# Down products of two expert layers, part of them in three rounded passes, in a four-layer transformer block on one Trainium2 core

## The chip, the cores and the metric

The kernel runs on one core of one Trainium2 chip. The time is the device time of one execution in microseconds (us). The core's engines are TensorE (PE in the rows; PEld is its weight load), VectorE (DVE), ScalarE (ACT), GpSimd (POOL) and SyncE (SP, which issues most of the transfers). Each engine runs its own instructions in the order in which they were written; engines wait for each other through semaphores only.

## The reference, cut to what matters

The input x is 4 batches of 512 tokens of 128 features, all in float32. Four layers follow each other, each added to x behind a layer norm:

```python
x = x + L0_xattn(layernorm(x), ctx, ctx)   # 16 heads of 8, 154 context rows
x = x + L0_ffn(layernorm(x))               # 8 experts, hidden width 512, top 2, gelu
x = x + L1_xattn(layernorm(x), ctx)        # self attention, cross attention, feed forward, three norms
x = x + L1_ffn(layernorm(x))               # 32 experts, hidden width 64, top 6, silu(g) * u, one shared expert
```

In the first expert layer every expert is computed for every token: `h = gelu(x W1 + b1)`, `y = h W2`, and the outputs are summed with the routing weights, which are zero for experts that were not chosen. In the second one `o = (silu(x Wg) * (x Wu)) Wd`, also for every expert, weighted in the same way. The products with `W2` and `Wd` are the down products.

## The kernel before, in words

The work of one batch is four stages: A (first attention), B (first expert layer), C (second attention with its feed forward) and D (second expert layer). Batches are interleaved: stage A of all four runs first, then B of one batch beside C of the batch before, then D beside what is left of C and D's own router. All products keep features on partitions and the 512 tokens along the free dimension, so that a 128x512 float32 tile fills one PSUM bank.

The order of each engine's instructions is taken from five tables, `PLAN_SP`, `PLAN_POOL`, `PLAN_ACT`, `PLAN_DVE` and `PLAN_PE` (lines 107 to 331). Each names a part of the work (a generator such as `gelus` or `downs`), a batch, and a start for each of its steps; `merged` (L38) writes the steps down in order of these starts. Nothing at run time looks at the starts: they fix the order within an engine, and the semaphore waits do the rest. A planner outside the kernel made the tables.

**Stage B** has 32 chunks of 128 hidden features (`NC0`), four for each expert. For chunk c, `first` (L1655) multiplies by W1 in three passes of a rounded type, `fp32r`: the weights and the input were each split into a rounded high part and the remainder (`product3`, L1491: high by high, low by high, high by low; lines 1493, 1494, 1495 in the rows). The result is in bank 0 or 1. `gelus` (L901, row L911) on ScalarE writes it into one of four slots of `h32`. `second` (L1673, row L1681) multiplies the slot by a 128x128 block of `w2s` in plain float32, accumulating the four chunks of an expert in bank 2. VectorE multiplies bank 2 by the routing weights `WB`, which a transfer spread over all partitions (`stage_b`, L1245, tile `ty`), and GpSimd adds the result to `acc_o` (L776).

**Stage D** has 17 chunks (`ND`): the shared expert and 16 pairs of experts. `gates` (L1825) makes two three-pass products, gate into bank 0 and up into bank 1. ScalarE takes silu of bank 0 into `s32`, two slots (`stage_d`, L1002). VectorE multiplies it by bank 1 into a slot of `h32` (L1445), and for chunks 1 to 16 multiplies the slot by the combine weights `CB` (L1451). `downs` (L1840, row L1851) multiplies by `dns`, or `shd` for chunk 0, in plain float32, and accumulates all 17 chunks in bank 2. Then comes a copy to SBUF, a transposition, the addition of x and the store.

Banks 0 and 1 are claimed anew for each chunk, so that TensorE's next product into bank 1 waits for L1445 of the chunk before.

**Stage C** and the routers are chains of many small steps. A norm (class `Norm`) is, on VectorE, four statistics (L395), four aggregates (L399), then, behind two GpSimd steps (L424, and the power at L427), four steps of 128x4 (L403, L406, L409, L412) and four 128x128 scalings (L418). All of VectorE's work, that of stage D too, stands in one queue with these.

GpSimd's own work is small before the change: the power steps, the sums of stage B, a bias sum (L786) and the low halves of the second layer's gate and up weights (`split1`, L748).

Of the kernel before, what the change touches and what calls it, by code (L numbers as in the profile page):

```python
# [25 lines left out]
F32 = mybir.dt.float32  # L26
F32R = mybir.dt.float32r
U8 = mybir.dt.uint8
ALU = mybir.AluOpType
# [62 lines left out]
class Signal:  # L92
# [6 lines left out]

    def then(self):  # L100

        return Signal(self.sem, self.per, self.at(NB, 0))
# [5 lines left out]
    "constants": [[6, 1272, 10975]],  # L108
    "load_x": [[0], [1040], [2704], [5590]],
    "load_context": [[1260], [4711], [7811]],  # L110
    "second_weights": [[14389, 14395, 28061, 38108, 39646, 41268]],
    "load_context1": [[14407], [24876], [31482], [35078]],
    "store": [[48439], [50521], [56182], [57613]],
    "spread_first": [[13617, 13859, 14401, 14945, 15567, 16098, 16858, 17511, 18133], [18975, 19217, 19342, 20142,
        21401, 22143, 23263, 23892, 24870], [26203, 26446, 26452, 27125, 28055, 28944, 30116, 30829, 31476], [32967,
        33210, 33216, 33959, 35072, 35774, 37822, 38062, 38535]],
    "spread_second": [[37816, 38084, 38096, 38541, 38553, 40408, 40666, 41025, 41256, 41444, 41808, 42078, 42388,
# [4 lines left out]
}  # L122
PLAN_POOL = {
    "constants": [[0, 15, 32, 60, 289, 340, 368]],
    "norm_a": [[710, 737], [1818, 1845], [3788, 3815], [7460, 7487]],
    "values": [[1946], [5119], [8117], [11089]],
    "key_tails": [[1983, 3916], [4316, 5058], [8157, 8218], [9729, 11027]],
    "norm_b": [[6000, 6027], [13177, 13204], [18984, 19787], [26163, 26191]],
    "stage_b": [[14945, 15567, 16098, 16858, 17511, 18133, 18858, 19342], [21045, 21401, 22143, 23263, 24803, 24939,
# [204 lines left out]
def build_program(nc, a):  # L334
# [5 lines left out]
    def sig(name, per):  # L340
        return Signal(ctx.enter_context(nc.semaphore(name)), per)
# [1599 lines left out]
```

## Time and profile before

| | |
|---|---|
| median of 3 runs | 597.2 us (596.64 to 597.66) |
| the profiled execution | 596.67 us |
| its span, first to last instruction | 594.9 us |
| TensorE busy | 569.7 us (96%) |
| VectorE busy | 401.7 us (68%) |
| ScalarE busy | 322.5 us (54%) |
| GpSimd busy | 105.4 us (18%) |
| transfers | 38.35 MB, 64 GB/s in the mean |

Matmuls are pipelined and their recorded ends are modelled: a row of TensorE starts with the weight load's end and overlaps the next. What a pass costs is read from start to start, or from the chain of waits, which counts each stretch once. A plain float32 product of 128x512 appears as two records, a three-pass product as three. VectorE rows may overlap a little as well.

### The profile page before, as it was taken

The numbers are of one execution on the slowest core, as the hardware profiler recorded it, in microseconds if no ns is written. First come the engines' busy times: TensorE is split into PE (matmuls) and PEld (weight loads), VectorE is DVE, ScalarE is ACT, GpSimd is POOL, SyncE is SP. The second block draws the span as 40 slices with busy tenths as digits, with TensorE's granted clock in tenths as the row PEclk, the third lists the DMA queues.
The fourth block names the chain that finished last, engine by engine and source line by source line (L and its number), as shares of the span: only waits on it lengthen the run. The fifth ranks groups of instructions, "written<-read, shape, count | busy, mean of one in ns | idle before, by whom it ended". The sixth has DMA issues, their size and how long they took to land.

```text
span 594.9 us, 8098 instructions
## 1 busy us (share of the span) xinstructions
PE 569.7 (96%) x2512; PEld 374.7 (63%) x2512; DVE 401.7 (68%) x1265; ACT 322.5 (54%) x566; POOL 105.4 (18%) x120
## 2 busy tenths in 40 slices
PE   4899999999999999999999899999899999999997
PEld 3556666665566667656676466666666676666664
DVE  6888989774132344666637585777889999768564
ACT  1587688766454476644855348745292542342321
POOL 3111110000111311242202432126201110100000
PEclk9999999999999999999999999999899999999999
DMA  4400000300311100101111011061321233341431
GB/s 119 195 15 10 18 10 2 105 39 19 107 36 35 54 20 19 36 28 54 60 31 44 14 42 44 1 199 39 122 75 51 90 119 98 111 138 62 143 120 56
DMA packets 23306, 38.35 MB, mean 64 GB/s; under 512 B 3776, under 2 KB 9536, under 8 KB 22880
## 3 DMA queue, kind: packets, MB, share of 16 engines
q1 hardware_dynamic: 22832, 37.44, 19.9%
q8 instruction: 20, 0.33, 0.2%
q10 hardware_dynamic: 432, 0.40, 0.2%
q14 instruction: 22, 0.18, 0.1%
HBM read 36.45 MB, written 1.38 MB: 64 GB/s over the span
## 4 chain that ended last, share of the span: by engine, by line
PE 80%; DVE 10%; ACT 4%; issue 2%; POOL 2%; DMA 1%; DVEq 0%; POOLq 0%; ACTq 0%
PE ps L1681 16%; PE ps L1493 9%; PE ps L1495 9%; PE ps L1851 9%; PE ps L1494 9%; PE ps L1488 3%; PE ps L1568 3%; PE ps L1588 3%; PE ps L1500 3%; PE ps L1603 2%; PE ps L1600 2%; PE ps L1758 1%; PE ps L1738 1%; DVE NM L1156 1%; PE ps L1530 1%
## 5 line engine op out<-in xcount | busy, mean ns | idle before, releaser
L1493 PE MATMUL ps<-xThi,w1s 128*128 128x512 f32 x256 | 147.5, 576 | 2.9 <-DVE h L1445 2.6
L911 ACT ACTIVATE h<-ps,early 128x512 f32<-128x512 f32 x128 | 86.7, 687 | 88.8 <-PE ps L1495 68.9
L1681 PE MATMUL ps<-h,w2s 128*128 128x512 f32 x256 | 122.5, 594 | 3.3 <-DVE ty L1245 3.2
L1495 PE MATMUL ps<-xTlo,w1s 128*128 128x512 f32 x256 | 101.4, 396 | 0.0
L1494 PE MATMUL ps<-xThi,w1s 128*128 128x512 f32 x256 | 100.9, 394 | 0.0
L1002 ACT ACTIVATE s<-ps 128x512 f32<-128x512 f32 x68 | 40.7, 598 | 95.4 <-PE ps L1495 93.8
L1493 PEld LDWEIGHTS ps<-xThi,w1s 128*128 128x128 f32 x256 | 48.5, 190 | 37.3 <-issue 18.2
L1681 PEld LDWEIGHTS ps<-h,w2s 128*128 128x128 f32 x256 | 46.2, 189 | 35.5 <-issue 23.8
L1494 PEld LDWEIGHTS ps<-xThi,w1s 128*128 128x128 f32 x256 | 48.7, 190 | 28.6 <-issue 24.3
L776 POOL TENSOR_TENSOR acc_o<-acc_o,ty 128x512 f32<-128x512 f32 x32 | 41.9, 1310 | 140.2 <-DVE ty L1245 115.7
L1445 DVE TENSOR_TENSOR h<-s,ps 128x512 f32<-128x512 f32 x68 | 46.5, 684 | 28.2 <-PE ps L1495 21.0
L1851 PE MATMUL ps<-h,w2s 128*128 128x512 f32 x128 | 63.5, 592 | 0.0
L1156 DVE TENSOR_REDUCE NM<-ps 128x2 f32<-128x308 f32 x128 | 56.1, 471 | 10.5 <-PE ps L1568 9.2
L1245 DVE TENSOR_TENSOR ty<-ps,WB 128x512 f32<-128x512 f32 x32 | 22.0, 686 | 53.4 <-PE ps L1681 53.4
L1495 PEld LDWEIGHTS ps<-xTlo,w1s 128*128 128x128 f32 x256 | 48.3, 189 | 11.2
L1451 DVE TENSOR_TENSOR h<-h,CB 128x512 f32<-128x512 f32 x64 | 44.2, 690 | 1.0
L1568 PE MATMUL ps<-KS,QS 128*128 128x320 f32 x128 | 41.8, 375 | 2.2 <-DVE NM L1156 1.4
L864 ACT ACTIVATE h<-ps 128x512 f32<-128x512 f32 x54 | 31.1, 597 | 10.8 <-PE ps L1588 9.7
L1568 PEld LDWEIGHTS ps<-KS,QS 128*128 128x128 f32 x128 | 23.6, 194 | 18.4 <-DVE NM L1156 9.7
L1851 PEld LDWEIGHTS ps<-h,w2s 128*128 128x128 f32 x128 | 23.8, 189 | 11.1 <-issue 5.3
L1588 PE MATMUL ps<-QS,KS 128*128 128x512 f32 x64 | 26.2, 440 | 0.4
L798 ACT ACTIVATE QS<-ps 128x512 fp32r<-128x512 f32 x32 | 18.4, 596 | 11.3 <-PE ps L1500 11.0
(264 smaller groups left out, 889.6 us busy)
## 6 DMA issues: line engine op xcount, KB each, us to landing
CB<-ct_rows SPq DMA_DIRECT2D x128, 128.0 KB, 2.9
WB<-wt_rows SPq DMA_DIRECT2D x32, 256.0 KB, 3.2
w2s<-w_dram SPq DMA_DIRECT2D x2, 2048.0 KB, 8.5
raw<-gu_dram SPq DMA_DIRECT2D x4, 512.0 KB, 3.8
x_in<-x_dram SPq DMA_DIRECT2D x4, 256.0 KB, 2.9
w2s<-dn_dram SPq DMA_DIRECT2D x1, 1024.0 KB, 5.7
out_dram<-ty SPq DMA_DIRECT2D x4, 256.0 KB, 2.9
late<-late_dram SPq DMA_DIRECT2D x1, 608.5 KB, 7.5
```

What stands on the lines that cost most here:

```text
L776: nc.gpsimd.tensor_tensor(acc_o[:], acc_o[:], ty[:, e % 2, :], ALU.add).then_inc(b_acc.sem, 1)
L911: nc.scalar.activation(h32[:, c % HR, :], bank[c % 2], ACT.Gelu, bias=b1T[:, c:c + 1]).then_inc(b_gelu.sem, 1)
L1156: V.tensor_reduce(NM[:, i, h:h + 2], src, AX.X, ALU.max, negate=True).then_inc(a_nm.sem, 1)
L1445: V.tensor_tensor(h, s32[:, (b * ND + n) % 2, :], bank[1], ALU.mult).then_inc(d_t.sem, 1)
L1451: V.tensor_tensor(h, h, CB[:, slot, :], ALU.mult).then_inc(d_h.sem, 1)
L1493: M(dst, w[0], xThi[:, x, :], start=start, stop=False)
L1494: M(dst, w[1], xThi[:, x, :], start=False, stop=False)
L1495: return M(dst, w[0], xTlo[:, x, :], start=False, stop=stop)
L1568: M(bank[u % 2][:, 0:2 * KW], QS[:, g, i * P:(i + 1) * P], KS[:, g, 2 * half:2 * half + 2, :].rearrange("p h k -> p (h k)"), start=True, s ...
L1588: M(bank[k], lhs, QS[:, g, :], start=True, stop=True).then_inc(a_s_ps.sem, 1)
L1681: M(bank[2], w2s[:, c * P:(c + 1) * P], h32[:, c % HR, :], start=(c % 4 == 0), stop=(c % 4 == 3)).then_inc(b_y.sem, 1)
L1851: M(bank[2], w, h32[:, (b * ND + n) % HR, :], start=(n == 0), stop=(n == ND - 1)).then_inc(d_dn.sem, 1)
```

## The change

The down products of chunks 1, 3, 5, ... of stage B and all down products of stage D are made in three passes of rounded parts instead of one plain float32 product. Even chunks of stage B stay as they were.

For that the hidden tile is split each time: ScalarE copies the 128x512 slot of `h32` into a rounded tile (`highs_b`, `highs_d`; two slots each), and GpSimd subtracts it from the slot, in place, into the remainder (`lows_b`, `lows_d`). The down product waits for the remainder instead of for gelu or for the combine weights. The down weights are split once in the same way: for stage B the odd blocks (`split2`, two pieces of 1024 columns), for stage D the shared block and four pieces of 512 columns (`split3`).

No large tile is added for the high halves: `hh0` (stage B) lies in the memory of `s32`, `hh1` (stage D) in that of `WB`, the low parts in that of `h32`, `w2s` and `shd` themselves (`twins`). So the first silu of stage D waits for the last down product of stage B, and the first high half of stage D for the last use of `WB`. The semaphores are those of parts that ended, counted on.

All five plan tables are replaced by new ones, with the new steps in them; they are left out here. In the new order of TensorE in the last batch of stage D, the down product of chunk n-3 stands behind the gate and up products of chunk n; before it was that of chunk n-2.

```diff
+    def twins(name, shape):
...
+        with nc.sbuf_tensor(name, shape, F32) as plain:
+            pass
+        return plain, sb(name + "_r", shape, F32R)
...
-    h32 = sb("h32", [P, 4, S])
+    h32, h32r = twins("h32", [P, 4, S])
...
-    w2s = sb("w2s", [P, NC0 * P])
+    w2s, w2r = twins("w2s", [P, NC0 * P])
...
+    w2h = sb("w2h", [P, NP1 * P], F32R)
...
-    WB = sb("WB", [P, 2, S])
-    s32 = sb("s32", [P, 2, S])
+    WB, hh1 = twins("WB", [P, 2, S])
+    s32, hh0 = twins("s32", [P, 2, S])
...
+        def split2():
+            for k in range(2):
+                yield
+                pool.wait_ge(w2_hi.sem, w2_hi.at(0, k + 1))
...
+        def lows_b(b):
+            for j in range(NC0 // 2):
+                yield
+                pool.wait_ge(b_hi.sem, b_hi.at(b, j + 1))
+                o = (2 * j + 1) % HR
+                nc.gpsimd.tensor_tensor(h32r[:, o, :], h32[:, o, :], hh0[:, j % 2, :].bitcast(F32), ALU.subtract).then_inc(b_lo.sem, 1)
+
+        def lows_d(b):
+            for n in range(ND):
+                yield
+                t = b * ND + n
+                pool.wait_ge(d_hi.sem, d_hi.at(b, n + 1))
+                nc.gpsimd.tensor_tensor(h32r[:, t % HR, :], h32[:, t % HR, :], hh1[:, t % 2, :].bitcast(F32), ALU.subtract).then_inc(d_lo.sem, 1)
...
+        def highs_b(b):
+            for j in range(NC0 // 2):
+                yield
+                act.wait_ge(b_gelu.sem, b_gelu.at(b, 2 * j + 2))
+                if b or j >= 2:
+                    act.wait_ge(b_y.sem, b_y.at(b, 2 * j - 2))
+                copy(hh0[:, j % 2, :], h32[:, (2 * j + 1) % HR, :]).then_inc(b_hi.sem, 1)
+
+        def highs_d(b):
+            for n in range(ND):
+                yield
+                t = b * ND + n
+                if n:
+                    act.wait_ge(d_h.sem, d_h.at(b, n))
+                else:
+                    act.wait_ge(d_t.sem, d_t.at(b, 1))
+                if t >= 2:
+                    act.wait_ge(d_dn.sem, d_dn.at(b, n - 1))
+                else:
+                    act.wait_ge(b_ty.sem, b_ty.at(NB - 1, E0))
+                copy(hh1[:, t % 2, :], h32[:, t % HR, :]).then_inc(d_hi.sem, 1)
...
+                else:
+                    act.wait_ge(b_y.sem, b_y.at(NB, 0))
                 nc.scalar.activation(s32[:, (b * ND + n) % 2, :], bank[0], ACT.Silu).then_inc(d_silu.sem, 1)
...
+        def down3(dst, w, x, start, stop):
+            (whi, wlo), (xhi, xlo) = w, x
+            M(dst, whi, xhi, start=start, stop=False)
+            M(dst, wlo, xhi, start=False, stop=False)
+            return M(dst, whi, xlo, start=False, stop=stop)
...
-                pe.wait_ge(b_gelu.sem, b_gelu.at(b, c + 1))
-                M(bank[2], w2s[:, c * P:(c + 1) * P], h32[:, c % HR, :], start=(c % 4 == 0), stop=(c % 4 == 3)).then_inc(b_y.sem, 1)
+                j, at, ends = c // 2, c % 4 == 0, c % 4 == 3
+                if c % 2:
+                    pe.wait_ge(b_lo.sem, b_lo.at(b, j + 1))
+                    if b == 0 and j % 8 == 0:
+                        pe.wait_ge(w2_lo.sem, w2_lo.at(0, j // 8 + 1))
+                    w = w2h[:, j * P:(j + 1) * P], odd_low[:, j, :]
+                    down3(bank[2], w, (hh0[:, j % 2, :], h32r[:, c % HR, :]), at, ends).then_inc(b_y.sem, 1)
+                else:
+                    pe.wait_ge(b_gelu.sem, b_gelu.at(b, c + 1))
+                    M(bank[2], w2s[:, c * P:(c + 1) * P], h32[:, c % HR, :], start=at, stop=ends).then_inc(b_y.sem, 1)
...
-                w = shd[:] if n == 0 else dns[:, (n - 1) * P:n * P]
-                M(bank[2], w, h32[:, (b * ND + n) % HR, :], start=(n == 0), stop=(n == ND - 1)).then_inc(d_dn.sem, 1)
+                if b == 0 and (n == 0 or n % 4 == 1):
+                    pe.wait_ge(dn_lo.sem, dn_lo.at(0, 1 + (n + 3) // 4))
+                pe.wait_ge(d_lo.sem, d_lo.at(b, n + 1))
+                c, t = slice((n - 1) * P, n * P), b * ND + n
+                w = (w2h[:, c], dn_low[:, c]) if n else (shh[:], sh_low[:])
+                down3(bank[2], w, (hh1[:, t % 2, :], h32r[:, t % HR, :]), n == 0, n == ND - 1).then_inc(d_dn.sem, 1)
```

## Rows read from the trace of the kernel before

**Rows 1.** Busy time of each engine, share of the span, instructions.

```profile
PE 569.7 (96%) x2512; PEld 374.7 (63%) x2512; DVE 401.7 (68%) x1265; ACT 322.5 (54%) x566; POOL 105.4 (18%) x120
```

**Rows 2.** The chain of waits, 560 to 595 us: start, length, what.

```profile
561.28 0.23 PE ps L1493
561.51 0.23 PE ps L1494
561.75 0.23 PE ps L1495
...
564.91 0.86 PE ps L1851 x2
...
567.15 0.86 PE ps L1851 x2
...
587.38 2.70 PE ps L1851 x6
590.10 0.61 ACT acc_o L798
```

**Rows 3.** Busy time by stretch, all engines: length, then busy and instructions of each.

```profile
135.00:197.00 62.00, 61.46 (x228) 36.87 (x229) 15.58 (x56) 33.17 (x51) 10.52 (x10) 1.00 0.16 49
197.00:266.00 69.00, 67.95 (x285) 44.27 (x284) 36.54 (x121) 41.89 (x73) 17.51 (x17) 1.00 0.10 32
...
461.00:508.00 47.00, 46.54 (x202) 32.64 (x201) 43.94 (x135) 19.84 (x36) 5.44 (x7) 1.00 0.32 97
508.00:550.00 42.00, 42.00 (x162) 28.35 (x161) 31.13 (x87) 14.57 (x23) 1.61 (x2) 1.00 0.35 110
```

**Rows 4.** Groups by line and shape, whole span: busy, mean ns, idle before.

```profile
L798 ACT ACTIVATE QS<-ps 128x512 fp32r<-128x512 f32 x32 | 18.4, 596 | 11.3 <-PE ps L1500 11.0
...
L1451 DVE TENSOR_TENSOR h<-h,CB 128x512 f32<-128x512 f32 x64 | 44.2, 690 | 1.0
```

**Rows 5.** GpSimd's groups by shape, 197 to 461 us.

```profile
L776 POOL TENSOR_TENSOR acc_o<-acc_o,ty 128x512 f32<-128x512 f32 x25 | 32.9, 1317 | 92.8 <-DVE ty L1245 68.3 <-ACT acc_o L798 24.4
...
L748 POOL TENSOR_TENSOR w1s<-raw,w1s 128x1024 fp32r<-128x1024 f32 x4 | 9.9, 2487 | 25.0 <-ACT w1s L798 25.0
...
L786 POOL TENSOR_TENSOR norm2b<-norm,late_rows 128x512 f32<-128x512 f32 x3 | 3.8, 1276 | 5.9 <-DVE norm L1255 5.9
```

**Rows 6.** Timeline, all engines, 417 to 422 us.

```profile
417.43 2.38 POOL L748 TENSOR_TENSOR w1s<-raw,w1s 128x1024 fp32r<-128x1024 f32 x1
417.49 2.34 DVE L403 TENSOR_TENSOR ln_c_t<-ln_c_y 128x4 f32<-128x4 f32 x1 [0.18 <-POOL ln_c_y L427]
...
419.87 0.16 DVE L406 TENSOR_TENSOR ln_c_t<-ln_c_t,ln_c_ve 128x4 f32<-128x4 f32 x1
...
421.35 0.79 PE L1493 MATMUL ps<-xThi,w1s 128*128 128x512 f32 x1 [1.68 <-DVE h L1445]
```

**Rows 7.** The chain of waits, 412 to 426 us.

```profile
422.14 0.43 PE ps L1494
422.57 0.43 PE ps L1495
```

**Rows 8.** Timelines of VectorE, then of GpSimd, from 218.5, 266, 444 and 482.5 us.

```profile
218.74 2.06 DVE L418 TENSOR_SCALAR xn<-X,ln_b_mv,ln_b_t 128x128 f32<-128x128 f32 x4
...
445.41 1.89 DVE L1388 TENSOR_TENSOR sfc<-sc,late_rows 128x128 f32<-128x128 f32 x1
...
482.96 0.69 DVE L1445 TENSOR_TENSOR h<-s,ps 128x512 f32<-128x512 f32 x1
483.87 0.95 DVE L1451 TENSOR_TENSOR h<-h,CB 128x512 f32<-128x512 f32 x1
...
482.98 1.29 POOL L786 TENSOR_TENSOR norm2b<-norm,late_rows 128x512 f32<-128x512 f32 x1 [6.39 <-DVE norm L1255]
...
266.52 1.65 POOL L776 TENSOR_TENSOR acc_o<-acc_o,ty 128x512 f32<-128x512 f32 x1 [4.04 <-DVE ty L1245]
```

**Rows 9.** Who TensorE waited for, 197 to 461 us: total, times, longest.

```profile
PE ps L1681 <- DVE ty L1245: 3.2, 2, 2.1
PE ps L1493 <- DVE h L1445: 2.6, 2, 1.7
PE ps L1777 <- DVE PN L1317: 0.4, 1, 0.4
```

More of the change, by code:

```diff
@@ L107 @@
 PLAN_SP = {
[L108 to L116, printed above, removed]
@@ L258 @@
+    "halves_d": [[35274, 37351], [42230, 43094], [45447, 48114], [50279, 50379]],
+    "router": [[35761, 35793, 35825, 35867, 36042, 36240, 36272, 36323, 36391, 36494, 36526, 36558, 36805, 36825],
[3 rows of a table added]
+    "stage_d": [[39385, 39551, 39673, 39738, 39917, 39980, 40052, 40301, 40423, 40489, 40560, 40696, 41114, 41179,
[8 rows of a table added]
 }
 PLAN_PE = {
-    "context_keys": [[720], [1948], [5240], [8257]],
-    "context_values": [[1150], [4648], [7748], [10485]],
-    "inputs": [[1040, 1237], [2576, 3058], [5600, 6147], [8706, 9088]],
@@ L316 @@
[L316 to L317 removed]
[8 rows of a table removed]
[L326 removed]
[4 rows of a table removed]
+    "context_keys": [[720], [1825], [5405], [8261]],
+    "context_values": [[1150], [4626], [7736], [10507]],
+    "inputs": [[1040, 1239], [2644, 3072], [5234, 6123], [8387, 9133]],
@@ new lines @@
+    "output": [[5329, 5530], [8456, 8656], [11246, 11515], [14086, 14280]],
+    "prepare_b": [[11367, 12094, 13507], [14828, 16240, 19114], [21734, 23034, 24559], [28414, 28779, 30083]],
+    "first": [[13367, 13856, 14131, 14208, 14533, 14602, 14757, 14996, 15065, 15223, 15515, 15584, 15810, 15879, 16103,
[8 rows of a table added]
+    "weights": [[13997], [20919], [26816], [32818]],
+    "second": [[14375, 14464, 14671, 14928, 15137, 15292, 15360, 15446, 15656, 15742, 15948, 16034, 16401, 16487,
[8 rows of a table added]
+    "stage_c": [[14884, 17507, 19217, 20062, 20246, 21479], [26332, 26700, 26905, 26991], [33220, 33296, 33458, 34502]
+        , [39175, 40326, 40521, 41811]],
@@ L434, in build_program @@
     w1s = sb("w1s", [P, 2, NC0 * P], F32R)
-    w2s = sb("w2s", [P, NC0 * P])
+    w2s, w2r = twins("w2s", [P, NC0 * P])
     w1raw = w2s
-    gus, dns = w1s, w2s[:, 0:NP1 * P]
+    w2h = sb("w2h", [P, NP1 * P], F32R)
+    odd, odd_low = (w.rearrange("p (c two k) -> p c two k", two=2, k=P)[:, :, 1, :] for w in (w2s[:], w2r[:]))
+    gus, dns, dn_low = w1s, w2s[:, 0:NP1 * P], w2r[:, 0:NP1 * P]
     shs = sb("shs", [P, 2, 2 * P], F32R)
-    shd = sb("shd", [P, P])
+    shd, sh_low = twins("shd", [P, P])
+    shh = sb("shh", [P, P], F32R)
     lg = sb("lg", [P, NT, E0])
@@ L911, in gelus, with split2, split3 @@
                 nc.scalar.activation(h32[:, c % HR, :], bank[c % 2], ACT.Gelu, bias=b1T[:, c:c + 1]).then_inc(b_gelu.sem, 1)
+        def split2():
+            for k in range(2):
+                yield
+                act.wait_ge(down0_loaded.sem, 16)
+                c = slice(1024 * k, 1024 * k + 1024)
+                copy(w2h[:, c].rearrange("p (c k) -> p c k", k=P), odd[:, 8 * k:8 * k + 8, :]).then_inc(w2_hi.sem, 1)
+        def split3():
+            for k in range(NDN):
+                yield
+                w, hi, _, chunks = down1_piece(k)
+                act.wait_ge(down1_loaded.sem, 32)
+                if chunks:
+                    act.wait_ge(b_y.sem, b_y.at(NB - 1, chunks))
+                copy(hi, w).then_inc(dn_hi.sem, 1)
+        def highs_b(b):
+            for j in range(NC0 // 2):
+                yield
+                act.wait_ge(b_gelu.sem, b_gelu.at(b, 2 * j + 2))
[4 more added lines that the diff above has]
+            for n in range(ND):
+                yield
+                t = b * ND + n
[8 more added lines that the diff above has]
+                copy(hh1[:, t % 2, :], h32[:, t % HR, :]).then_inc(d_hi.sem, 1)
         def stage_c(b):
```

258 lines of the change are left out of this document (139 added, 119 removed), and 196 rows, old and new, of tables (PLAN_ACT, PLAN_DVE, PLAN_PE, PLAN_POOL).

## The prediction

> **What bounds the kernel now.** I read the busy times first: TensorE stands at 96%, the next engine at 68% [rows 1]. That share is of modelled, overlapping records, so I went to the chain of waits for the true pace. In its last 35 us nearly everything is TensorE: a plain float32 down product takes 0.86 us, each of the three rounded passes 0.23 us, so three passes 0.69 us, and two down products that follow each other (564.91 and 567.15) are 2.24 us apart, which is 0.86 + 2 x 0.69 with nothing left over [rows 2]. TensorE alone bounds the last stage. By stretches the other engines have room in places: VectorE is busy for 15.6 of 62 us in the first stage B, for 36.5 of 69 in the next with stage C beside it, for 43.9 of 47 in the second stage D with the end of C and a router beside it, and for 31.1 of 42 in the third [rows 3]. Last I looked at what TensorE waits for from 197 to 461 us: VectorE, in few but long waits [rows 9]. Two of the longest lead to one cause, and it decides this prediction.
>
> **That cause.** At 417.43 GpSimd begins a subtraction of 2.38 us that reads SBUF. VectorE's next step, a product of 128x4 elements in SBUF, begins at 417.49 and lasts 2.34 us; the one behind it, of the same size, takes 0.16 us. VectorE's queue is held, stage D's product L1445 stands in it, bank 1 stays taken, and TensorE is idle for 1.68 us [rows 6]. Its passes then take 0.43 instead of 0.23 us until 424 us [rows 7]: the granted clock fell from the level of 2.4 GHz to that of 1.2 GHz behind the idle time, which costs another 6 x 0.2 + 0.2 = 1.4 us. So one GpSimd instruction cost the end some 3 us. It isn't alone: a scaling group of four lasts 2.06 us where four undisturbed ones last 1.1, a 128x128 sum 1.89 us [rows 8]. Going through VectorE's instructions from 197 to 461 us I find 18 (these two groups hold the first and nearly the last, 218.74 to 445.41) that are longer than others of their line and shape, together by 17.0 us, each beside one of 32 GpSimd instructions that read large tiles: 25 sums, four subtractions of 1024 columns, three bias sums [rows 5]. That is 0.53 us of VectorE for each such GpSimd instruction. The Trainium skill has this as a rule (SBUF — State Buffer, Who interferes with whom): a VectorE instruction with two SBUF inputs and a GpSimd instruction that reads SBUF want the same port pair, and the later one blocks until the other is done. The trace agrees, with 2.34 against 0.16 us. By the same rule an instruction that has one input in PSUM is spared, and the trace agrees there too: L1445 took its usual 0.69 us beside GpSimd's bias sum, while L1451 behind it, both inputs in SBUF, took 0.95 [rows 8]. Without the rule's spared instructions the sum below would be worse.
>
> **The change, part by part.** The sum is made against the profiled execution (596.67 us, span 594.9); the median is 0.5 us above it, so differences are added to 597.2.
>
> TensorE: 64 down products in stage B (16 odd chunks, 4 batches) and 68 in stage D (17, 4 batches) go from 0.86 to 3 x 0.23 us. 132 x 0.165 = 21.8 us less.
>
> ScalarE: 132 copies into a rounded tile at 0.60 us [rows 4], 79 us, and some 6 us for the weights. From 322.5 it comes to about 408 of 600 us [rows 1]; beside B and C it has 41.9 of 69 us, with 16 copies 51.5 [rows 3]. It is covered in the steady part: nothing. If it weren't, a late gelu or silu would cost up to 0.6 us each time.
>
> GpSimd: 132 subtractions of 128x512. The nearest row is the bias sum and the sums at 1.28 to 1.32 us [rows 5]. So 170 us, and the weights' seven, of which two of 1024 columns at 2.4 us, about 10. From 105 to 285 us: it has the time, its port is the question.
>
> The way from the hidden tile to its down product grows by a copy and a subtraction, 0.60 + 1.28 and two waits of 0.05 to 0.1, some 2.0 us. In the steady part of stage D the new order puts the down product three chunks behind, and one chunk is 3 x 0.69 = 2.07 us of TensorE, so this is hidden. It shows at the end: now TensorE makes its last three down products back to back from 587.38 [rows 2]; then the last waits for copy and subtraction. 2.0 less 0.17: +1.9 us. At the start of stage B the first odd chunk is late by as much, with other work in front: between 0 and 2, I take 1. Stage D can't have its first silu until stage B's last down product is done, since both use one memory; stage C's products are there to fill: between 0 and 2, I take 1. The splitting of the weights lies before both and off TensorE: 0. Without the port this gives -21.8 + 1.9 + 1 + 1 = -17.9 us.
>
> The port: stage B of the first batch (VectorE a quarter busy) and stage D of the last (no C beside it) I count as nothing. In the latter a chunk asks the port for L1451, 0.69, and a subtraction, 1.28: 1.97 of 2.07 us, and rows overlap a little at their ends, so it fits. This leaves 48 subtractions of stage B, 51 of stage D and five of the weights, 104, in stretches where VectorE has chains of steps. At 0.53 us each they hold VectorE for 55 us more. What of this reaches the end? Before, 17.0 us of holding went with 7.0 us of TensorE's waits between 197 and 461 us (the three largest rows are 6.2 of them [rows 9]) and the 1.4 us of slow clock: a share of 0.5. So 55 x 0.5 = +27.5 us. Bounds: if only waits as long as the two longest count (3.8 us of 17, a share of 0.22), +12; if VectorE has no room left, as in the second stage D where it already has 43.9 of 47 us, the share goes towards 0.8, +44. I take 0.5, which is measured on the kernel that is nearest, and since slack that absorbs one hold is used up by the next I see no reason to go lower. The other direction, GpSimd held by VectorE, is 0.33 us (1.65 in [rows 8] against 1.32 in the mean [rows 5]), a sixth of a chunk; I take it as covered by the distance of three chunks.
>
> Sum: -17.9 + 27.5 = +9.6, so 606.8 us.
>
> **The rivals.** *Cover holds (faster).* The holds fall into VectorE's idle time, the orders are new and might put the steps of C away from the subtractions. For it: 18 holds led to only four or five visible waits. Against: semaphores, not the order, decide when a subtraction meets a step, and a norm's power step stands on GpSimd itself, so that a subtraction queued right behind it starts exactly when VectorE's next step does, as at 417.43. With a share of 0.1 the price is 5.5: 597.2 - 17.9 + 5.5 = 584.8 us. It decides the sign from a share of 17.9 / 55 = 0.33 downwards.
>
> *VectorE becomes the bound beside C and the routers (slower still).* In the second stage D VectorE would have 43.9 us of work and 17 holds in 43 us of TensorE's. If in the first two stages D each of 34 subtractions holds it for 0.8 us and all of it counts, +27, with the other 70 as above, 70 x 0.53 x 0.5 = +18.5: 597.2 - 17.9 + 45.7 = 625 us. For it: 43.94 of 47 [rows 3]. Against: a part of these holds hits queues with nothing urgent.
>
> *The late halves decide.* Each odd down product waits for its subtraction by 0.3 us because GpSimd's queue also holds sums and power steps of 1.3 and 1.0 us in front of it, and TensorE finds nothing behind it in its own queue: 99 x 0.3 = 30 us on top of -17.9, without port holds: 609 us. Near my number with another cause; the waits view tells them apart.
>
> **How the numbers follow.** My forecast has a chance of 0.57 (its own range 600 to 618), late halves 0.07, VectorE as the bound 0.12, cover holds 0.19, and 0.05 that price and saving cancel. What a measurement can tell from no change is 0.2%, 1.2 us. Faster 0.19, same 0.05, slower 0.76. The range goes from 588 (a share of 0.16) to 625 (the second rival) and leaves out most of "cover holds" and the far end of the second.
>
> **What would show it.** Right: in the last stage D down products are 2.07 to 2.1 us apart; GpSimd is near 285 us; VectorE's small steps (L403, L406, L409, L1388) have means several times 0.16 us, L1451 in stages D with C beside it is over 0.8 us in the mean, and VectorE's busy time rises by some 50 us over 401.7 though no work is added to it; TensorE's waits name VectorE's L1445 and L1245, and the clock falls in more places than one. Wrong: small steps keep their lengths; or they grow and TensorE's waits stay near 7 us from 200 to 460, then the cover holds and the kernel is faster; or three passes of the mixed operands take more than 0.69 us, which no row of before shows for a moving tile written by GpSimd.

## The result and the profile after

The changed kernel takes 636.69 us in the median of four runs (636.22 to 637.21), the kernel before 596.93 in four runs beside it: a ratio of 1.0664, with a 95% interval of 1.0646 to 1.0682, or 39.7 us more. The forecast was 606.8, its range 588 to 625: the sign was right, the size was not, and the time lies outside the range.

First the page of the changed kernel, busy times and granted clock. They answer to [rows 1].

```profile
PE 565.9 (89%) x2644; PEld 399.1 (63%) x2644; DVE 470.9 (74%) x1265; ACT 398.9 (63%) x703; POOL 289.4 (46%) x259
...
PEclk9899999999999999999999999988999989899999
```

TensorE has 3.8 us less to do and falls from 96% to 89% of the span. The 3.8 is not the price of the passes: records at half the clock are longer, and there are more of them now. VectorE has 69 us more, with as many instructions (1265) as before: nobody gave it work. The groups show where it went (line, engine, operation, tile, count; busy, mean ns; idle before).

```profile
L830 POOL TENSOR_TENSOR h_r<-h,WB_r 128x512 fp32r<-128x512 f32 x68 | 93.0, 1377 | 76.5 <-ACT WB_r L880 76.2
L823 POOL TENSOR_TENSOR h_r<-h,s_r 128x512 fp32r<-128x512 f32 x64 | 82.3, 1288 | 104.1 <-ACT s_r L880 104.0
...
L1574 DVE TENSOR_TENSOR h<-h,CB 128x512 f32<-128x512 f32 x64 | 59.2, 925 | 1.2
...
L1568 DVE TENSOR_TENSOR h<-s,ps 128x512 f32<-128x512 f32 x68 | 46.3, 680 | 12.0 <-PE ps L1618 9.5
...
L438 DVE TENSOR_TENSOR ln_n_t<-ln_n_y 128x4 f32<-128x4 f32 x12 | 8.3, 688 | 8.7 <-POOL ln_n_y L462 8.7
...
L453 DVE TENSOR_SCALAR normed<-a,ln_n_mv,ln_n_t 128x128 f32<-128x128 f32 x48 | 24.7, 568 | 0.1
```

L823 and L830 are the new subtractions. L1574 is L1451 of [rows 4]: 690 ns there, 925 here. A product of four columns, L438 (before L403), has a mean of 688 ns; before it had 294, and [rows 6] has an undisturbed step of this size at 0.16 us. L1568 (before L1445), which takes one input from PSUM, keeps its 680 ns.

The stretches come next: length, busy time and count of TensorE, its weight load, VectorE, ScalarE and GpSimd, clock, DMA. They are the four stages B and then the four stages D; [rows 3] has the first two and the sixth and seventh of before.

```profile
140.00:198.00 58.00, 55.84 (x232) 38.13 (x231) 17.48 (x44) 40.88 (x63) 31.52 (x26) 1.00 0.13 42
198.00:266.00 68.00, 63.30 (x292) 44.85 (x292) 42.94 (x110) 47.36 (x87) 33.52 (x30) 1.00 0.13 40
266.00:336.00 70.00, 67.00 (x305) 47.18 (x304) 44.22 (x144) 48.85 (x88) 40.04 (x38) 1.00 0.14 42
336.00:420.00 84.00, 72.22 (x315) 49.69 (x314) 62.14 (x178) 55.23 (x95) 45.40 (x41) 0.96 0.20 66
420.00:489.00 69.00, 55.70 (x258) 41.23 (x257) 64.22 (x158) 41.30 (x76) 40.98 (x33) 0.98 0.15 46
489.00:545.00 56.00, 47.46 (x209) 35.58 (x208) 53.74 (x122) 26.41 (x43) 27.67 (x22) 0.95 0.28 89
545.00:588.00 43.00, 40.61 (x172) 29.56 (x172) 38.77 (x88) 24.48 (x40) 24.22 (x19) 0.99 0.32 99
588.00:635.00 47.00, 40.68 (x173) 30.45 (x171) 31.18 (x38) 22.79 (x38) 26.80 (x20) 0.99 0.32 101
```

The same points of the program in both traces: the first product of each of the four stages B and of the four stages D (taken where its second weight load starts), and the end.

```
          B0     B1     B2     B3     D0     D1     D2     D3     end
before  139.7  197.0  265.6  330.4  405.2  460.8  507.8  549.1  594.9
after   140.5  198.3  266.3  336.3  420.1  488.8  545.2  588.4  635.2
later     0.8    1.3    0.7    5.9   14.9   28.0   37.4   39.3   40.3
```

The first two stages B give back what the holds take. The loss of 36.7 us falls from the third stage B to the end of the second stage D. VectorE is busy there for 44.2 us of 70, then for 62.1 of 84, 64.2 of 69 and 53.7 of 56. The two stages that the forecast counted as free of holds, the first B and the last D, lose 0.5 and 1.0 us, but they aren't free of them: in the last stage D eight of VectorE's 16 combine products (L1574) take 1.1 to 1.7 us instead of 0.69.

What a hold looks like, at its worst (timeline, all engines, 428.5 to 434.5 us):

```profile
428.27 1.28 POOL L857 TENSOR_TENSOR acc_o<-acc_o,ty 128x512 f32<-128x512 f32 x1 [1.13 <-DVE ty L1368]
428.77 3.58 DVE L453 TENSOR_SCALAR normed<-a,ln_n_mv,ln_n_t 128x128 f32<-128x128 f32 x4
429.50 1.29 POOL L816 TENSOR_TENSOR w2s_r<-w2s,w2h 128x512 fp32r<-128x512 f32 x1
430.75 1.26 POOL L830 TENSOR_TENSOR h_r<-h,WB_r 128x512 fp32r<-128x512 f32 x1
...
432.27 0.68 DVE L1568 TENSOR_TENSOR h<-s,ps 128x512 f32<-128x512 f32 x1
433.00 0.72 PE L1616 MATMUL ps<-xThi,w1s 128*128 128x512 f32 x1 [1.99 <-DVE h L1568]
```

Three large reads of GpSimd stand back to back: an old sum, a weights' subtraction, a new one. Four scalings, 1.12 us when nothing disturbs them (at 7.91 us in the trace of before), take 3.58. Stage D's product is behind them in VectorE's queue, and TensorE idles for 1.99 us. Behind this idle the granted clock is 0.5 (the level of 1.2 GHz) for 3.4 us. Apart from the last microseconds of the span that is so six times, at 20.1, 395.6, 412.6, 433.1, 508.2 and 542.3 us; before it was so once, at 421.3 [rows 7]. The stretch at 20.1 us lies ahead of all new work. The others begin near the end of idles of 1.8 to 3.9 us. Not every such idle is followed by one:

```profile
451.02 0.50 PE L1616 MATMUL ps<-xThi,w1s 128*128 128x512 f32 x1 [2.42 <-DVE h L1568]
451.36 0.40 PE L1617 MATMUL ps<-xThi,w1s 128*128 128x512 f32 x1
```

Behind 2.42 us of idle the next pass has its 0.40 us here; in the slow stretch from 433.1 us the same line has 0.63.

Who TensorE waited for over the whole span (total, times, longest):

```profile
PE ps L1616 <- DVE h L1568: 17.7, 18, 2.4
...
PE ps L1818 <- DVE ty L1368: 5.2, 2, 3.9
PE ps L1611 <- DVE xn L453: 5.2, 1, 5.2
...
PE ps L1628 <- POOL h_r L830: 2.9, 7, 1.1
PE ps L1628 <- POOL h_r L823: 1.9, 4, 0.7
```

L1568 led two waits of 2.6 us before [rows 9]; now 18 of 17.7 us. The new subtractions themselves (L830, L823) are waited for only 4.8 us.

A measure used below is the held time: for each VectorE instruction, what it takes beyond the usual for its operation and shape, where that is over 0.08 us, summed over the span. It is 18.5 us before (25 instructions) and 95.1 after (111). Some 5 us of the 95.1 have nothing to do with the subtractions: in the new orders a fill of 2560 columns on GpSimd stands at 8.02 us beside two small VectorE steps. That part is in every kernel below that has the new orders.

### The profile page after: what moved, and what is told of

Same layout as the page of the kernel before. It is cut to its first block, busy times and chain, and to the rows that moved or that the text cites. A ratio compares the mean times of both kernels' runs of the same rounds, so it can differ in the third digit from the quotient of the medians.

```text
span 635.2 us, 8780 instructions
## 1 busy us (share of the span) xinstructions
PE 565.9 (89%) x2644; PEld 399.1 (63%) x2644; DVE 470.9 (74%) x1265; ACT 398.9 (63%) x703; POOL 289.4 (46%) x259
## 3 DMA queue, kind: packets, MB, share of 16 engines
HBM read 36.45 MB, written 1.38 MB: 60 GB/s over the span
## 4 chain that ended last, share of the span: by engine, by line
PE 51%; DVE 30%; issue 7%; ACT 6%; POOL 5%; DMA 1%; POOLq 0%; ACTq 0%; DVEq 0%
PE ps L1616 6%; PE ps L1618 5%; PE ps L1617 5%; PE ps L1818 5%; PE ps L1611 3%; DVE h L1568 3%; PE ps L1717 3%; PE ps L1628 3%; PE ps L1697 3%; DVE h L1574 2%; PE ps L1629 2%; PE ps L1630 2%; DVE normed L453 2%; DVE xn L453 2%; DVE NM L1279 2%
## 5 line engine op out<-in xcount | busy, mean ns | idle before, releaser
L1616 PE MATMUL ps<-xThi,w1s 128*128 128x512 f32 x256 | 118.7, 463 | 20.5 <-DVE h L1568 17.7
L823 POOL TENSOR_TENSOR h_r<-h,s_r 128x512 fp32r<-128x512 f32 x64 | 82.3, 1288 | 104.1 <-ACT s_r L880 104.0
L830 POOL TENSOR_TENSOR h_r<-h,WB_r 128x512 fp32r<-128x512 f32 x68 | 93.0, 1377 | 76.5 <-ACT WB_r L880 76.2
L1617 PE MATMUL ps<-xThi,w1s 128*128 128x512 f32 x256 | 101.5, 397 | 0.0
L1818 PE MATMUL ps<-h,w2s 128*128 128x512 f32 x128 | 67.0, 605 | 5.3 <-DVE ty L1368 5.2
L880 ACT ACTIVATE WB_r<-h 128x512 fp32r<-128x512 f32 x68 | 42.5, 629 | 45.0 <-DVE h L1574 23.7
L1368 DVE TENSOR_TENSOR ty<-ps,WB 128x512 f32<-128x512 f32 x32 | 22.0, 687 | 52.0 <-PE ps L1630 52.0
L1574 DVE TENSOR_TENSOR h<-h,CB 128x512 f32<-128x512 f32 x64 | 59.2, 925 | 1.2
L1568 DVE TENSOR_TENSOR h<-s,ps 128x512 f32<-128x512 f32 x68 | 46.3, 680 | 12.0 <-PE ps L1618 9.5
L1630 PE MATMUL ps<-h_r,w2h 128*128 128x512 f32 x128 | 50.8, 397 | 0.0
L1628 PE MATMUL ps<-s_r,w2h 128*128 128x512 f32 x64 | 41.8, 653 | 1.9 <-POOL h_r L823 1.9
L880 ACT ACTIVATE s_r<-h 128x512 fp32r<-128x512 f32 x64 | 40.2, 633 | 1.3
L946 ACT ACTIVATE h<-ps 128x512 f32<-128x512 f32 x54 | 30.8, 597 | 11.5 <-PE ps L1717 10.7
```

The costliest lines, as they stand in the source:

```text
L823: nc.gpsimd.tensor_tensor(h32r[:, o, :], h32[:, o, :], hh0[:, j % 2, :].bitcast(F32), ALU.subtract).then_inc(b_lo.sem, 1)
L830: nc.gpsimd.tensor_tensor(h32r[:, t % HR, :], h32[:, t % HR, :], hh1[:, t % 2, :].bitcast(F32), ALU.subtract).then_inc(d_lo.sem, 1)
L880: return nc.scalar.activation(dst, src, ACT.Copy)
L1568: V.tensor_tensor(h, s32[:, (b * ND + n) % 2, :], bank[1], ALU.mult).then_inc(d_t.sem, 1)
L1574: V.tensor_tensor(h, h, CB[:, slot, :], ALU.mult).then_inc(d_h.sem, 1)
L1616: M(dst, w[0], xThi[:, x, :], start=start, stop=False)
```

## The experiments

The theory in all of them is that GpSimd's new reads hold VectorE, and a part of the holds reaches the end. The rivals are the longer way to a down product, TensorE's passes costing more than 0.69 us, the new orders, ScalarE. Each kernel is compared with the kernel before on the same chip; a difference between two kernels is that of their ratios, times 597 us, and is sure to about 1.5 to 2 us by the intervals given.

Several runs missed the range that was expected of the theory. e1, e2, e5, e7 and e8 came out slower than it, and e4 did too; e3 came out 11 us faster. e1 fell into the range of the rival on ScalarE and the orders, and e8 into that of its rival; e12 fell between both ranges. So the misses say two things: the holds cost less than the 58 us that these expectations gave them, and the rest of the change gains less than 17.9. The later runs take that rest apart.

### The reads taken away, and their time put back without them

e1 leaves the 132 subtractions out and gives the high half to the third pass; e2 keeps their slots with fills that read nothing.

```diff
 e1  -  ("lows_b", map(lows_b, every)), ("lows_d", map(lows_d, every)),
     -  pe.wait_ge(d_lo.sem, d_lo.at(b, n + 1))
     +  pe.wait_ge(d_hi.sem, d_hi.at(b, n + 1))
 e2  -  nc.gpsimd.tensor_tensor(h32r[...], h32[...], hh1[...], ALU.subtract)
     +  three nc.gpsimd.memset of 512, 256 and 512 columns of the same slot
```

> The changed kernel without GpSimd's 132 subtractions: the down product waits for the rounded copy, and its third pass multiplies the high half a second time, so the remainder of the hidden tile is left out. Everything else stays, the 132 copies on ScalarE and the weights' splitting too. Theory P (holds at the port GpSimd shares with VectorE cost 58 us, and the rest of the change is worth the 17.9 us forecast): 578 to 585 us, VectorE busy about 402 to 410 us. Theory L (the longer way through copy and subtraction costs, not the port): 578 to 590 as well, since the longer half of the way is gone. Theory S (the gain of TensorE is eaten by ScalarE's copies, the shared memories or the new orders): over 592 us.

> The changed kernel with each subtraction replaced by three fills of the same slot on GpSimd, 512, 256 and 512 columns of zeros, behind one another: GpSimd is as long at it (fills of 1280 columns in the first kernel's rates are about 1.1 to 1.3 us) and the down product waits as before, but nothing reads SBUF. The remainder of the hidden tile is zero, that is left out. Theory P: 580 to 592 us, VectorE's L1574 back at 0.69 us (if fills hold the port too, as they write through it: some 610 or more with the same long VectorE steps). Theory L: 625 to 640 us, since the way is as long and GpSimd's queue as full.

e1: 594.49 us, ratio 0.9965 (0.9949 to 0.998), held 35.9. e2: 599.39, ratio 1.0037 (1.0013 to 1.0062), held 43.1. In e2 the way is about as long as in the changed kernel, GpSimd as busy (293.5 us for 289.4), the passes the same. Groups of e2:

```profile
L822 POOL MEMSET h_r<- 128x512 f32 x132 | 69.7, 528 | 137.8 <-ACT s_r L889 89.2 <-ACT WB_r L889 48.3
...
L1583 DVE TENSOR_TENSOR h<-h,CB 128x512 f32<-128x512 f32 x64 | 44.4, 693 | 1.2
```

L1583, the line of 925 ns in the changed kernel, is back at 693. But the fills are no clean stand-in, since they hold other VectorE steps. A scaling of four columns takes 0.57 us instead of 0.17 beside one, while the product ahead of it takes its 0.16:

```profile
525.42 0.16 DVE L441 TENSOR_TENSOR ln_d_t<-ln_d_t,ln_d_ve 128x4 f32<-128x4 f32 x1
525.62 0.57 DVE L444 TENSOR_SCALAR ln_d_t<-ln_d_t 128x4 f32<-128x4 f32 x1
525.63 0.53 POOL L825 MEMSET h_r<- 128x512 f32 x1
```

Most such steps of e2 are scalings like it (44 of 51, L453 above all), and what they take beyond their usual length is some 12 us of the 43.1 held. So the 4.3 us between e1 and e2 are the longer step and the fills' own holds together. The reads cost 37.4 us against fills and at most 41.7 against nothing (e1): either way the loss is the reads.

### The reads alone, in the kernel before

e3 puts 132 subtractions into the kernel before, from constant tiles into a tile that nobody reads.

```diff
+ def sub():
+     pool.wait_ge(made.sem, count[0] + 1)
+     nc.gpsimd.tensor_tensor(apart[:], part[:, 0, :], part[:, 1, :], ALU.subtract)
+ # after each odd gelu of stage B and each h of stage D
```

> The kernel before with 132 subtractions of 128x512 on GpSimd, in a tile of their own, each released by the gelu or the combine product that releases the copy in the changed kernel; nobody waits for them. No part of the reference is left out. Theory P: 640 to 660 us, since the holds are the same and no TensorE time is saved. Theory L and S: 597 to 601 us.

629.26 us, ratio 1.0536 (1.0516 to 1.0556), held 70.3. Its groups:

```profile
L760 POOL TENSOR_TENSOR apart<-part 128x512 f32<-128x512 f32 x132 | 171.2, 1297 | 127.0 <-DVE h L1478 71.3 <-ACT h L938 52.9 <-DVE h L1472 1.8
...
L1478 DVE TENSOR_TENSOR h<-h,CB 128x512 f32<-128x512 f32 x64 | 50.6, 791 | 1.0
...
L405 DVE TENSOR_TENSOR ln_n_t<-ln_n_y 128x4 f32<-128x4 f32 x12 | 11.5, 961 | 6.9 <-POOL ln_n_y L429 6.8
```

Work whose result nobody uses and for which nobody waits costs 32.0 us. Nothing of the change's orders, passes or copies is in this kernel.

### One stage at a time

e5 has the three passes in stage B alone, e6 in stage D alone (with the first silu's wait for stage B's last down product).

```diff
 e5  (stage D)  - down3(bank[2], w, (hh1[...], h32r[...]), ...)
                + M(bank[2], w, h32[:, (b * ND + n) % HR, :], ...)
 e6  (stage B)  - down3(bank[2], w, (hh0[...], h32r[...]), at, ends)
                + M(bank[2], w2s[:, c * P:(c + 1) * P], h32[:, c % HR, :], start=at, stop=ends)
```

> The changed kernel with stage D's down products in plain float32 as before (no copies, no subtractions, no splitting for them); stage B's odd chunks in three passes. Nothing of the reference is left out. Before this run: the first run without subtractions came to 594.5, with fills to 599.4, subtractions alone in the kernel before to 629.3 us. Theory P2 (holds cost by number of subtractions met by chains of VectorE; the splitting for stage D holds it too): the loss up to the first gate of stage D was 15 us with the new orders, stage D comes back to its old length: 608 to 616 us. Rival (the loss is made in stage B and only shows later): over 622.

> The changed kernel with stage B's down products all in plain float32 (no copies, no subtractions, no splitting for them); stage D in three passes, its first silu still behind the last product of stage B. Nothing of the reference is left out. Theory P2: stage B comes back to its old length, stage D keeps its loss of 25 us: 618 to 626 us. Rival: under 610.

e5: 617.7 us, ratio 1.0351 (1.0336 to 1.0367), held 57.6. e6: 621.56, ratio 1.0412 (1.0392 to 1.0433), held 67.3. That is +21.0 and +24.6; less, once, the 3.6 us that the orders cost by themselves (e12 below), since both kernels have them, their sum is 42.0, near the whole loss of 39.7. The change loses in either stage, though each saves TensorE work.

### The subtractions in halves, and on VectorE

e4 issues each subtraction as two of 256 columns; e8 moves all 132 to VectorE, behind the same copies.

```diff
 e4  + for H in (slice(0, S // 2), slice(S // 2, S)):
     +     nc.gpsimd.tensor_tensor(h32r[:, o, H], h32[:, o, H], hh0[:, j % 2, H], ALU.subtract)
 e8  - nc.gpsimd.tensor_tensor(...)
     + V.tensor_tensor(...)
```

> The changed kernel with each subtraction in two of 256 columns. Theory P: VectorE takes its turn between the two, so a hold lasts 0.55 us at most instead of 1.2; added holds of 77 us fall to about 40, their price of 58 us to about 30: 604 to 620 us. Theory P with holds that follow each other (VectorE doesn't get in between): 632 to 640. Theory L: 637 to 645, the way is longer by one instruction's start.

> The changed kernel with the 132 subtractions on VectorE, at the same places of the order; the splitting of the weights stays on GpSimd. Nothing is left out. No holds, a shorter way (0.69 instead of 1.28 us), but 91 us more work for VectorE, which then is busy for about 505 us. Theory P2: it fits in stage B and in the last two stages D, and in the first two, where VectorE has little room, it costs 12 to 20 us: 600 to 612 us. Rival (VectorE's queue is as harmful by its length as by the holds): over 625 us.

e4: 628.95 us, ratio 1.0518 (1.0484 to 1.0552), held 75.4. Its groups:

```profile
L833 POOL TENSOR_TENSOR h_r<-h,WB_r 128x256 fp32r<-128x256 f32 x136 | 111.7, 847 | 52.8 <-ACT WB_r L884 52.3
...
L1578 DVE TENSOR_TENSOR h<-h,CB 128x512 f32<-128x512 f32 x64 | 54.1, 845 | 1.2
```

8.7 us come back. The halves take 847 ns each in the mean, 1.69 us a pair against 1.38. A part of that is the second start (a piece of 256 columns takes 0.70 us in e15 below, 1.4 a pair); that the rest is GpSimd held in its turn fits, but no run separates it. e8: 626.53 us, ratio 1.0505 (1.0478 to 1.0532). VectorE is busy for 491.2 us, its products are undisturbed again at 685 ns, and TensorE waits for it all the same, in 24 small waits (404 to 595 us):

```profile
PE ps L1619 <- DVE h L1570: 11.4, 24, 1.0
...
PE ps L1614 <- DVE xi L455: 6.2, 1, 6.2
```

There is no room for 132 subtractions on VectorE; doing the work itself makes it busy for 89 us more than before, and that is still some 10 us better than being held by GpSimd doing it.

### The other parts of the sum, one by one

e12 keeps the new orders and the wait of the silu, with plain float32 products and no splitting. e7 is e1 without the weights' subtractions too. e13 is e7 without the 132 copies on ScalarE (gelu and combine write the rounded type). e11 is e7 with the last gate/up subtraction planned 14 us later in GpSimd's order.

```diff
 e7   -  ("split2", [split2()]), ("split3", [split3()]),   # GpSimd
 e13  -  ("highs_b", ...), ("highs_d", ...),               # ScalarE
 e11  -  "split1": [[28779, 36441, 38096, 40631, 40998]],
      +  "split1": [[28779, 36441, 38096, 40631, 42400]],
```

> Every down product in plain float32 as before, no copies, no subtractions, no splitting of down weights, but all five new orders and stage D's first silu still behind the last product of stage B. Nothing of the reference is left out. So far the kernel without any added GpSimd work has 589.5 us, 7.5 less than before where 17.9 were forecast. Theory N (the new orders and the memory sharing cost what is missing): 605 to 609 us. Theory C (the orders are neutral; ScalarE's copies and the longer way eat it): 596 to 600 us.

> The run without subtractions, and without those of the down weights too: all GpSimd work of the change is gone, the ScalarE copies of hidden tile and weights stay; every down product in question is made as three passes of the high halves, both remainders are left out. Theory P2 (seven subtractions of weights, four of them back to back with the gate and up weights' two, held one VectorE step for over 5 us and TensorE for 5.8): 582 to 588 us, and the stretch of the first stage D shorter by 6 to 8 us than in the run without subtractions. Rival S (ScalarE's copies, the shared memories or the new orders eat the gain of TensorE): 591 to 595 us, no change.

> The kernel without added GpSimd work, and without the 132 copies of hidden tiles on ScalarE too: gelu and the combine product write the rounded type themselves, and all three passes read it and the weights' high half; the remainders are left out. TensorE's work is that of the changed kernel. Theory N: 587 to 590 us, as with the copies. Theory C: 579 to 584 us.

> The kernel without added GpSimd work, with the last subtraction of the gate and up weights (1024 columns, was there before the change) 14 us later in GpSimd's order, so that it no longer runs back to back with the one before it; the remainders are left out as there. Theory N in this form (the new order put two of these holds side by side, where they hold the chain of stage C and TensorE waits 4.1 us): 584 to 587 us. Rival: 589 to 591, another hold takes its place.

| | us | ratio (95%) | held |
|---|---|---|---|
| e12 | 601.48 | 1.006 (1.0039 to 1.0081) | 29.7 |
| e13 | 583.99 | 0.9773 (0.9756 to 0.9791) | 29.7 |
| e7 | 589.45 | 0.9868 (0.9849 to 0.9887) | 30.7 |
| e11 | 585.51 | 0.9802 (0.9781 to 0.9822) | 29.8 |
| e1 | 594.49 | 0.9965 (0.9949 to 0.998) | 35.9 |

From e12 to e13 only the products differ in any large way (the copies of the down weights on ScalarE come with them): 17.1 us, where 132 x 0.165 gives 21.8. By stages, from first product to first product, e13 saves 2.6 us in the first stage B, as 16 x 0.165 asks, and nothing in the fourth (76.2 us for 75.5). The copies cost 5.7 (e7 against e13), the seven weights' subtractions 5.8 (e1 against e7). In e1 the old subtractions of 1024 columns follow a weights' subtraction without a gap, and three scalings last 5.83 us:

```profile
422.27 1.27 POOL L816 TENSOR_TENSOR w2s_r<-w2s,w2h 128x512 fp32r<-128x512 f32 x1 [0.55 <-ACT w2h L880]
422.38 5.83 DVE L453 TENSOR_SCALAR xi<-X,ln_c_mv,ln_c_t 128x128 f32<-128x128 f32 x3
423.50 4.63 POOL L800 TENSOR_TENSOR w1s<-raw,w1s 128x1024 fp32r<-128x1024 f32 x2
```

e7 has the two of 1024 columns back to back as well, beside the same norm, and TensorE's transposes wait for 4.09 us:

```profile
416.15 4.71 POOL L800 TENSOR_TENSOR w1s<-raw,w1s 128x1024 fp32r<-128x1024 f32 x2
...
422.50 0.75 PE L1610 MATMUL ps<-early,xi 128*128 128x128 f32 x4 [4.09 <-DVE xi L453]
```

e11 pulls them apart by one number: the wait falls to 2.0 us, the stretch at half the clock that stood behind it (at 422.9 us in e7) is gone, and 3.9 us are gained (ratios of 0.9868 and 0.9802).

### The change where little is held, and a version that beats both

The last stage D has little holding and no chain of stage C beside it. e10 is the kernel before with three passes only there, for 13 of its chunks, the copy ahead of the next silu on ScalarE and the down product two chunks behind. e14 puts the copy behind that silu and the down product three chunks behind. e15 is the kernel before with its old large reads in pieces. e16 is e14 with e15.

```diff
 e14  "downs" of the last batch:
      - 53811, 54035, 54442, 54666, ...
      + 53811, 54375, 54598, 54822, ...
 e15  + for o in range(0, w, 256):      # gate and up weights, was w = 1024 at once
      +     nc.gpsimd.tensor_tensor(dst[:, 1, c + o:c + o + 256], ...)
      + for H in (slice(0, S // 2), slice(S // 2, S)):      # the sums
      +     nc.gpsimd.tensor_tensor(acc_o[:, H], acc_o[:, H], ty[:, e % 2, H], ALU.add)
```

> The kernel before in its own orders, with three rounded passes in the last batch of stage D alone, chunks 1 to 13, where no chain stands beside on VectorE; the down weights are split in the stage D before, into memory that is free by then. Nothing is left out. Theory P: 13 x 0.165 = 2.1 us less, no long waits: 594.4 to 596.0 us. Rival (subtractions hold the combine products enough to take it back): 596.5 to 599 us.

> The kernel before with three rounded passes in the last batch of stage D alone, chunks 1 to 13, now with ScalarE's copy behind the silu of the next chunk and the down product behind the gate and up products three chunks later, as in the changed kernel. Nothing is left out. Theory P (no chain beside, so no price): 2.1 us less, 594.8 to 596.4 us. Rival (the subtraction holds the combine product also here, and one chunk takes over 2.24 us): 597.5 us or more.

> The kernel before with GpSimd's own old reads in pieces: the subtractions of gate and up weights in 256 columns instead of 1024, the 32 sums in two halves. Same orders, nothing is left out. Before, holds were 18.5 us, the longest 2.2 us, and the four places where TensorE fell behind together some 7 us. If the length of a single read sets the price: VectorE held for 8 to 12 us, no hold over 0.7, 592.5 to 595.5 us. Rival (VectorE doesn't get in between two pieces, or meets the next one at once): 596.5 to 598.5 us.

> The two kernels that beat the one before, together: three passes in the last batch of stage D for chunks 1 to 13, and GpSimd's old reads in pieces. Nothing is left out. If the two gains (0.27% and 0.37%) are independent, as one lies behind the other in time: 592.5 to 594.5 us. Rival (the second gain is not steady, its runs spread over 5 us): 595 to 597 us.

e10 was a miss: 604.3 us, ratio 1.0107 (1.0088 to 1.0126). A chunk takes 2.6 us instead of 2.07, in a ring that I had not counted: product, copy, then the silu of the next chunk behind the copy (timeline of e10, VectorE and ScalarE).

```profile
571.15 0.69 DVE L1496 TENSOR_TENSOR h<-h,CB 128x512 f32<-128x512 f32 x1
571.88 0.63 ACT L826 ACTIVATE WB_r<-h 128x512 fp32r<-128x512 f32 x1 [1.48 <-DVE h L1496]
572.41 0.58 ACT L1047 ACTIVATE s<-ps 128x512 f32<-128x512 f32 x1
```

e14 takes the ring away: 595.75 us, ratio 0.9973 (0.9964 to 0.9983). Its chain of waits has the same pass of three chunks 2.07 us apart, as three times 0.69 asks:

```profile
567.38 0.23 PE ps L1540
...
569.45 0.23 PE ps L1540
...
571.52 0.23 PE ps L1540
```

From the first product of the last stage D to its last up product e14 takes 35.4 us instead of 37.4, but one down product fewer stands in that stretch. To the end of the kernel it is 44.3 instead of 45.8 us: 1.5 us saved, and 1.6 by the ratio (1.0 to 2.1), where 13 x 0.165 = 2.1 was expected. e15: 594.97 us, ratio 0.9963 (0.9946 to 0.998), held 13.4. e16: 593.5 us in the median of 12 runs, ratio 0.9943 (0.9923 to 0.9962). It beats both kernels, by 3.4 us (2.3 to 4.6) the one before and by 43 the changed one. The gains over the kernel before are small, but the three intervals leave out 1; that e16 is faster than e15 or e14 alone isn't sure.

## Why the prediction was wrong

**The mechanism was right.** The forecast gave the plus to GpSimd's reads at the port. e2 and e3 show it from two sides: 37.4 us come with the reads when all else is there, 32.0 when nothing else is. Most of what was to show it does: L1568 and L1368 lead TensorE's waits on another engine, L438 of `ln_n` goes from 294 to 688 ns, L1574 is over 0.8 us, the clock falls in more places, GpSimd is at 289.4 for a forecast of 285. VectorE's busy time rises by 69 us where some 50 were named. Not every small step grew: L1388 (after L1511) had one hold of 1.6 us among its four before and fell from 688 to 408 ns in the mean, and the four L403 of `ln_c` fell from 974 to 430. The Trainium skill (SBUF — State Buffer, Who interferes with whom) spares an instruction with an input in PSUM, and L1568 at 680 ns agrees.

**The amount of holding came out right, partly by luck.** Forecast: 55 us for 104 reads, at 0.53 each, none for the other 28. Measured: 52 us between e2 and the changed kernel (95.1 less 43.1), 59.2 between e1 and it, 51.8 between e3 and before. That is 0.39 us for each of 132 reads (e2, e3), and the last stage D, set to nothing, has holds too: a lower price met more reads.

**The share was wrong, and this is the step that failed.** "I take 0.5, which is measured on the kernel that is nearest" made 27.5 us of it. Measured are 37.4 of 52, a share of 0.72, and 32.0 of 51.8, or 0.62, in e3. The bound of +44 with "the share goes towards 0.8" held it. Against e1 it is 41.7 of 59.2, 0.70. The half came from 18 holds in a kernel whose VectorE was busy for 68% of the span, without the new ones between them; that this is why it was too low is argued, not shown. The argument I had beside it, that slack which absorbs one hold is used up by the next, spoke for more than 0.5, and I used it only against less. The clock has a small part: e2 has four stretches of 3.4 us at half the clock before its last microseconds, the changed kernel six, so two more; 3.4 us at half the clock cost up to 1.7 us.

**"Without the port this gives ... -17.9" was wrong too.** e7, with everything but GpSimd's new work, gains 7.9 us, and the longer way takes 4.3 of them back. The parts, forecast and measured:

| part | forecast | measured | from |
|---|---|---|---|
| three passes on TensorE | -21.8 | -17.1 | e12 to e13 |
| new orders, shared memory | +2 | +3.6 | before to e12 |
| copies on ScalarE | 0 | +5.7 | e13 to e7 |
| weights' subtractions | 0, holds apart | +5.8 | e7 to e1 |
| longer way through GpSimd | +1.9 | +4.3 | e1 to e2 |
| the reads' holds | +27.5 | +37.4 | e2 to after |
| sum | +9.6 | +39.7 | |

The measured parts add up by construction, each is sure to about 1.5 to 2 us, and another order of taking things away could share them out otherwise. The 4.3 us contain the holds by e2's fills.

The forecast's 27.5 covered five of the weights' reads too, so its two parts compare as follows: holds 37.4 + 5.8 = 43.2 for 27.5, the rest -17.1 + 3.6 + 5.7 + 4.3 = -3.5 for -17.9. The miss of 30.1 us is half the holds, whose share was too low, and half the other four terms. The copies were set to nothing because ScalarE had room in the mean. It had (63% after), but a copy that stands ahead of a gelu or silu delays that one; e10 shows such a ring at 0.5 us a chunk. That this is what the 5.7 us in e7 are made of is argued, not shown. Of the weights' subtractions, that they would line up with the old ones of 1024 columns, beside a norm, was not seen. The order of GpSimd's queue could have shown it before any run.

Why TensorE's passes gain only 17.1 is not shown. It fits that a shorter product only lengthens a wait where TensorE waits for somebody: e13 saves what was forecast in the first stage B and nothing in the fourth, where it waits twice for VectorE (2.8 and 1.8 us). In the last stage D e14 saves 1.5 to 1.6 of 2.1 us.

**The last stage and the tail.** From the first product of the last stage D to its last up product it took 36.1 us after and 37.4 before, with 16 down products in either stretch: 1.3 saved instead of 16 x 0.165 = 2.6. The forecast had let combine product and subtraction fit side by side into a chunk; eight of 16 combine products are held there. From 604 us on the down products are 2.1 to 2.2 us apart. The tail from the last up product on is 10.7 for 8.4 us, +2.3 for a forecast of +1.9.

**The rivals.** *Cover holds* wanted a share of 0.1 and is out. *Late halves* is out as the cause: TensorE waits 4.8 us for subtractions, and e1 against e2 prices the way at 4.3 at most. It would have given 30. *VectorE becomes the bound* came nearest: 625 us, its place right (the second stage D with 53.74 of 56 us busy, the first with 64.22 of 69); its chance was 0.12. What it missed is the third and fourth stage B and the other rows of the table. The range ended at this rival's price although that price still contained the -17.9, which nothing had measured.

## What to carry to other kernels

Work given to an idle GpSimd is not free if it reads SBUF beside a busy VectorE: count the reads and multiply by the hold of one in the trace. In this kernel 0.6 to 0.75 of the new holds reached the end, once they were several times the old ones. Test it first by putting the same reads into the kernel before with nobody waiting; e3 gave 32.0 us for reads that cost 37.4 in the change. A saving on the bounding engine is worth its face value only in stages where that engine waits for nobody, and small steps set to zero because an engine has room need a look at what stands directly behind them in its queue.

## What the runs showed of the hardware

A VectorE instruction that is held gets its turn between two GpSimd instructions that follow each other without a gap. So it was with two of 1024 columns in e7 (4.71 us): two VectorE steps of 128x4 took 2.37 and 2.26 us, one for each. Pieces issued without a semaphore between them make the single hold shorter. In e15 the subtraction of [rows 6] comes in four pieces, and the small steps that waited 2.34 us take 0.7 each:

```profile
416.33 2.80 POOL L749 TENSOR_TENSOR w1s<-raw,w1s 128x256 fp32r<-128x256 f32 x4
416.39 0.70 DVE L403 TENSOR_TENSOR ln_c_t<-ln_c_y 128x4 f32<-128x4 f32 x1 [0.18 <-POOL ln_c_y L427]
417.12 0.66 DVE L406 TENSOR_TENSOR ln_c_t<-ln_c_t,ln_c_ve 128x4 f32<-128x4 f32 x1
417.82 0.65 DVE L409 TENSOR_SCALAR ln_c_t<-ln_c_t 128x4 f32<-128x4 f32 x1
```

Each of the three is held again by the next piece, so that a chain of small steps is held once per step: 2.01 us for the three, against 2.34 and 0.16 for the first two of before.

The holding goes both ways. Where a subtraction starts first, as at 598.77 us, VectorE's L1574 takes 1.73 us for 0.69. Where both start together, GpSimd can be the one that is held: two subtractions take 3.08 us instead of 2.6, and in the mean a subtraction in stage D has 1377 ns for 1288 in stage B.

```profile
589.36 0.69 DVE L1574 TENSOR_TENSOR h<-h,CB 128x512 f32<-128x512 f32 x1
589.36 3.08 POOL L830 TENSOR_TENSOR h_r<-h,WB_r 128x512 fp32r<-128x512 f32 x2 [1.29 <-ACT WB_r L880]
```

Fills on GpSimd (528 ns in the mean) leave VectorE's products of two SBUF inputs at their 693 ns, but hold scalings: L444 takes 0.57 us beside one in e2, and the four-column scaling at 8.49 us of the changed kernel takes 2.75 beside a fill of 2.23. Idles of TensorE of 1.8 to 3.9 us were followed by 3.4 us at half the clock five times in the changed kernel, and an idle of 2.42 us was not.
